# One transformer block on one core: scores of two head pairs joined, the last feed-forward columns packed, first values copied by ScalarE, orders laid anew

## What is computed

```python
scores = jnp.einsum('bqgre,bkge->bgrqk', q, k) / jnp.sqrt(jnp.float32(D_HEAD))
scores = jnp.where(causal_mask, jnp.float32(-1000000.0), scores)
probs = jax.nn.softmax(scores, axis=-1)
z = jnp.einsum('bgrqk,bkge->bqgre', probs, v)
...
h = h @ w1 + b1
a, g = jnp.split(h, 2, axis=-1)
h = a * jax.nn.gelu(g, approximate=False)
x = x + h @ w2 + b2
```

## Time and profile before

| | value |
|---|---|
| median of the runs | 1151.18 us |
| the profiled execution's own time | 1151.44 us |
| its span in the trace | 1149.6 us |
| TensorE instructions (matmul, weight load) | 17504, 17504 |
| granted TensorE clock, mean | 0.998 of full speed |
| VectorE, ScalarE, GpSimd busy | 1040.9, 1001.2, 958.5 us |

### The profile page before, as it was taken

The page is one execution under the profiler, slowest core; times in us unless marked ns, Lnnn a source line. Parts: engine busy times, 40 slices in busy tenths (PEclk is TensorE's granted clock), DMA queues, the critical chain, the costliest instruction groups (busy, mean ns, idle before and its releaser), DMA issues.

```text
span 1149.6 us, 45236 instructions
## 1 busy us (share of the span) xinstructions
PE 1132.4 (98%) x17504; PEld 820.2 (71%) x17504; DVE 1040.9 (91%) x4019; ACT 1001.2 (87%) x3168; POOL 958.5 (83%) x950
## 2 busy tenths in 40 slices
PE   9999999999999999999999999999999999999987
PEld 7677666777678676777676776777767777666765
DVE  7898899999999899999989899998998989999984
ACT  6888889888899889889898998989888898997795
POOL 2787888889888898888978889888978898988855
PEclk9999999999999999999999999999999999999999
DMA  6001010000110100111001101001001010011010
GB/s 233 11 12 33 16 32 22 21 16 9 31 27 5 45 14 3 41 25 39 14 3 36 38 23 32 17 4 42 9 23 26 4 28 23 14 35 29 11 33 27
DMA packets 31094, 31.85 MB, mean 28 GB/s; under 512 B 12576, under 2 KB 21408, under 8 KB 30752
## 3 DMA queue, kind: packets, MB, share of 16 engines
q1 hardware_dynamic: 30448, 28.17, 9.3%
q10 hardware_dynamic: 432, 0.79, 0.2%
HBM read 10.07 MB, written 2.10 MB: 11 GB/s over the span
## 4 chain that ended last, share of the span: by engine, by line
PE 83%; DVE 6%; POOL 5%; issue 2%; ACT 2%; DMA 0%; SPq 0%; POOLq 0%; DVEq 0%; ACTq 0%
PE psum L496 39%; PE psum L535 11%; PE psum L571 11%; PE psum L548 7%; PE psum L649 5%; PE psum L680 4%; PE psum L631 2%; PE psum L664 2%; DVE prob L898 1%; POOL x_hat L1164 1%; POOL rnorm L1135 1%; PE psum L594 1%; DVE b_prob L980 1%; ACT b_prob L803 1%; POOL b_prob L1152 1%
## 5 line engine op out<-in xcount | busy, mean ns | idle before, releaser
L747 ACT ACTIVATE prob<-prob,negmax 128x512 f32<-128x512 f32 (+3 forms) x512 | 282.7, 558 | 16.1 <-DVE negmax L898 15.3
L898 DVE CUSTOM_DVE_ANT_0 prob<-psum,causal 128x512 f32<-128x512 f32 (+3 forms) x512 | 224.0, 484 | 11.5 <-PE psum L535 9.6
L1102 POOL TENSOR_SCALAR prob<-prob,rowinv 128x384 f32<-128x384 f32 (+1 forms) x256 | 161.2, 649 | 50.1 <-DVE rowinv L904 48.7
L803 ACT ACTIVATE b_prob<-b_prob,b_negmax 128x128 f32<-128x128 f32 x512 | 199.0, 395 | 0.8 <-DVE b_negmax L980 0.7
L496 PE MATMUL psum<-wqkv,h_t 128*64 128x512 f32 x768 | 190.8, 599 | 0.1
L535 PE MATMUL psum<-k_t,q_t 64*128 64x384 f32 (+3 forms) x1024 | 163.5, 443 | 0.7 <-DVE prob_t L910 0.6
L1122 POOL TENSOR_TENSOR r<-r 128x512 f32<-128x512 f32 x120 | 153.4, 1284 | 7.0 <-DVE r L938 6.9
L571 PE MATMUL psum<-prob_t,v 128*64 128x256 f32 x1280 | 153.1, 380 | 0.0
L980 DVE CUSTOM_DVE_ANT_0 b_prob<-psum,band,rnorm 128x128 f32<-128x128 f32 x512 | 145.8, 344 | 5.4 <-PE psum L649 4.9
L1152 POOL TENSOR_TENSOR b_prob<-b_prob,b_rowinv 128x1024 f32<-128x1024 f32 x61 | 116.0, 1902 | 27.7 <-DVE b_rowinv L1000 27.6
L1105 POOL TENSOR_TENSOR prob<-prob,rowinv 128x512 f32<-128x512 f32 x96 | 98.1, 1047 | 36.4 <-DVE rowinv L904 36.3
(11 more groups left out here) (104 smaller groups left out, 2725.6 us busy)
## 6 DMA issues: line engine op xcount, KB each, us to landing
vb_mid<-vb SPq DMA_DIRECT2D x112, 128.0 KB, 2.4
x_t<-in_x_t SPq DMA_DIRECT2D x8, 256.0 KB, 3.9
x_n<-in_x SPq DMA_DIRECT2D x8, 256.0 KB, 3.1
x<-x SPq DMA_DIRECT2D x64, 31.8 KB
out<-x SPq DMA_DIRECT2D x15, 128.0 KB, 1.8
wqkv<-in_wqkv SPq DMA_DIRECT2D x1, 1536.0 KB, 11.3
w<-in_w SPq DMA_DIRECT2D x1, 768.0 KB, 13.1
x<-x SPq DMA_DIRECT2D x48, 0.2 KB
```

The source lines that it names most:

```text
L747: last = af(pr, pr, ACT.Exp, bias=negmax[:, k % 4, o:o + 1], scale=-1.0, accum_out=rowsum[:, k % 4, o:o + 1])
L803: last = af(pr, pr, ACT.Exp, bias=b_negmax[:, a, o:o + 1], scale=-1.0, accum_out=b_rowsum[:, a, o:o + 1])
L898: vec.tensor_tensor_reduce(prob[:, k % PROBS, h, p * K:(p + 1) * K], bank[:, p * K:(p + 1) * K], causal[:, S - K:S], -E ** -0.5, 3.0e38, A ...
L1102: last = gp.tensor_scalar(pr, pr, rowinv[:, k % 4, h:h + 1], 1.0, ALU.mult, ALU.mult)
```

## The change

Scores at i = 0 and i = 1 (`JOINT`): two head pairs, even and odd, share their keys. Of the last 64 keys only the tile's late 64 queries see any. The late queries of both pairs are copied side by side into a new tile `q_late`, and one product computes both against the last 64 keys. For each two pairs and row half there are now 3 products of 64 streamed columns at i = 0 (before: 2 of 128), and one of 192 and four of 64 at i = 1 (before: 2 of 256). All the products of one row half now come first, then those of the other. To make the outputs fit, the even pair's queries are projected with the tile's halves swapped, a second causal mask is stored, the maxima read the odd pair's blocks in another order, and `value` streams 128 columns for each pair instead of 256 for two.

Feed-forward: of the third chunk's 85 value columns, 64 are computed as one product whose two column halves take half of the tokens each, and the other 21 come out of the gate product, whose weights have room from column 96 on. `gate` of that chunk is three VectorE instructions.

`project_v` is copied out of PSUM by ScalarE. `q_late` takes one further copy on each of the two engines at i = 0 and 1. The lists of all engines, the banks and the `warm` counts are laid anew. Each step occurs as often as before, but for the `warm` steps (13 for 11, with 33 products for 34); the copy of `project_v` moves from VectorE's list to ScalarE's. In TensorE's list scores and turns of stage a now mostly alternate.

```diff
+REST = 96
...
 PROBS, PROB_TS, V_RING = 3, 4, 6
+JOINT = (0, 1)
...
-WARM = (3, 2, 2, 4, 2, 4, 3, 2, 1, 9, 2, )
+WARM = (2, 1, 1, 3, 4, 3, 3, 3, 2, 1, 5, 1, 4, )
...
-        causal = sb("causal", [P, S], BF16)
+        causal = sb("causal", [P, 2, S], BF16)
...
+        q_late = sb("q_late", [P, len(JOINT), CA // 2, P])
...
+        def even_at(i, p):
+
+            return p // 2 * 3 * E + E if i == 0 else 0
+
+        def odd_at(i, p, block):
+
+            return p // 2 * 3 * E if i == 0 else (6 - block) * E
+
+        def late_of(bank):
+
+            return bank.rearrange("p (d x n) -> p d x n", d=2, n=E)[:, :, ::3, :]
...
                 bank, = claim("a_q", b, i, h)
+                tokens = x_t[:, b % 2, i * P:(i + 1) * P]
+                turned_tokens = tokens.rearrange("p (q n) -> p q n", q=2)[:, ::-1, :]
                 for c in range(4):
-                    last = halves(bank[:, c * P:(c + 1) * P], wq[:, 4 * h + c, :], x_t[:, b % 2, i * P:(i + 1) * P])
+                    moving = turned_tokens if i in JOINT and c % 2 == 0 else tokens
+                    last = halves(bank[:, c * P:(c + 1) * P], wq[:, 4 * h + c, :], moving)
...
                 banks = claim("a_scores", b, i, c)
-                for p in range(np_):
+                queries = q_t[:, (NT * b + i) % 2, :, :]
+                for p in range(0, np_, 2 if i in JOINT else 1):
+                    keys = k_t[:, b % 2, (c + p) // 2, 0:K]
                     for h in range(2):
-                        last = mm(banks[h][:, p * K:(p + 1) * K], q_t[half(h), (NT * b + i) % 2, c + p, :],
-                                  k_t[half(h), b % 2, (c + p) // 2, 0:K], start=True, stop=True)
+                        if i not in JOINT:
+                            last = mm(banks[h][:, p * K:(p + 1) * K], queries[half(h), c + p, :], keys[half(h)], start=True, stop=True)
+                            continue
+                        even, odd = queries[half(h), c + p, :], queries[half(h), c + p + 1, :]
+                        both = q_late[half(h), i, (c + p) // 2, :]
+                        place = even_at(i, p)
+                        mm(banks[h][:, place:place + K - E], even, keys[half(h), 0:K - E], start=True, stop=True)
+                        mm(banks[h][:, place + K - E:place + K], both, keys[half(h), K - E:K], start=True, stop=True)
+                        for x in range(2 * i + 1):
+                            at = odd_at(i, p, x)
+                            last = mm(banks[h][:, at:at + E], odd, keys[half(h), x * E:(x + 1) * E], start=True, stop=True)
...
-                for p in range(0, max(np_, 2), 2):
+                for p in range(0, max(np_, 2), 1 if i in JOINT else 2):
                     for j in range(i + 1):
                         for h in range(2):
                             g = 2 * ((c + p) // 2) + h
-                            last = mm(bank[half(h), p * P:(p + 2) * P], v[:, (NT * b + j) % V_RING, g * E:(g + 1) * E],
-                                      two_pairs(k % PROB_TS, np_, i, h, p, j), start=(j == 0), stop=(j == i))
+                            values = v[:, (NT * b + j) % V_RING, g * E:(g + 1) * E]
+                            if i in JOINT:
+                                place, turned_probs = slice(p * P, (p + 1) * P), two_pairs(k % PROB_TS, np_, i, h, p - p % 2, j)[:, p % 2, :, :]
+                                if p % 2 == 0:
+                                    turned_probs = turned_probs[:, ::-1, :]
+                            else:
+                                place, turned_probs = slice(p * P, (p + 2) * P), two_pairs(k % PROB_TS, np_, i, h, p, j)
+                            last = mm(bank[half(h), place], values, turned_probs, start=(j == 0), stop=(j == i))
                 last.then_inc(valued, 1)
 
...
                 bank, = claim("b_ffn", l, g, ch)
-                for part in (1, 0):
-                    last = halves(bank[:, (1 - part) * z:(2 - part) * z], w1[:, l, part, ch * P:(ch + 1) * P], f_t[:, 0:z])
+                last = halves(bank[:, 0:z], w1[:, l, 1, ch * P:(ch + 1) * P], f_t[:, 0:z])
+                if ch < CH - 1:
+                    last = halves(bank[:, z:2 * z], w1[:, l, 0, ch * P:(ch + 1) * P], f_t[:, 0:z])
+                else:
+                    for w in range(2):
+                        last = mm(bank[half(w), z:z + z // 2], w1[:, l, 0, ch * P:ch * P + E], f_t[:, w * z // 2:(w + 1) * z // 2], start=True, stop=True)
                 last.then_inc(ffn_done, 1)
...
-                copy(q_t[:, (NT * b + i) % 2, 4 * h:4 * h + 4, :].rearrange("p c n -> p (c n)"), bank).then_inc(q_act, 1)
+                last = copy(q_t[:, (NT * b + i) % 2, 4 * h:4 * h + 4, :].rearrange("p c n -> p (c n)"), bank)
+                if i in JOINT:
+                    last = copy(q_late[:, i, 2 * h:2 * h + 2, :].rearrange("p d (x n) -> p d x n", n=E), late_of(bank))
...
+            def project_v(b, i):
+                act.wait_ge(v_done, nth("pe", "a_v", (b, i)))
+                bank, = banks_of("a_v", b, i)
+                copy(v[:, (NT * b + i) % V_RING, :], bank).then_inc(v_ready, 1)
...
-                vec.tensor_copy(q_t[:, (NT * b + i) % 2, 4 * h:4 * h + 4, :].rearrange("p c n -> p (c n)"), bank).then_inc(q_dve, 1)
-
-            def project_v(b, i):
-                dve.wait_ge(v_done, nth("pe", "a_v", (b, i)))
-                bank, = banks_of("a_v", b, i)
-                vec.tensor_copy(v[:, (NT * b + i) % V_RING, :], bank).then_inc(v_ready, 1)
+                last = vec.tensor_copy(q_t[:, (NT * b + i) % 2, 4 * h:4 * h + 4, :].rearrange("p c n -> p (c n)"), bank)
+                if i in JOINT:
+                    last = vec.tensor_copy(q_late[:, i, 2 * h:2 * h + 2, :].rearrange("p d (x n) -> p d x n", n=E), late_of(bank))
+                last.then_inc(q_dve, 1)
...
                 for p in range(np_):
                     o = h * np_ + p
-                    vec.tensor_tensor_reduce(prob[:, k % PROBS, h, p * K:(p + 1) * K], bank[:, p * K:(p + 1) * K], causal[:, S - K:S],
+                    masked, seen, mask = prob[:, k % PROBS, h, p * K:(p + 1) * K], bank[:, p * K:(p + 1) * K], causal[:, 0, S - K:S]
+                    if i in JOINT and p % 2 == 0:
+                        seen, mask = bank[:, even_at(i, p):even_at(i, p) + K], causal[:, 1, S - K:S]
+                    elif i in JOINT:
+                        masked, mask = masked.rearrange("p (x n) -> p x n", n=E), mask.rearrange("p (x n) -> p x n", n=E)
+                        if i == 0:
+                            seen = bank[:, even_at(0, p - 1) - E:even_at(0, p - 1) + K].rearrange("p (x n) -> p x n", n=E)[:, ::2, :]
+                        else:
+                            masked, mask = masked[:, ::-1, :], mask[:, ::-1, :]
+                            seen = bank[:, K - E:2 * K - E].rearrange("p (x n) -> p x n", n=E)
+                    vec.tensor_tensor_reduce(masked, seen, mask,
                                              -E ** -0.5, 3.0e38, ALU.add, ALU.min, negmax[:, k % 4, o:o + 1]).then_inc(max_ready, 1)
...
+            def gated(gelu, value, bias):
+
+                return vec.scalar_tensor_tensor(out=gelu, in0=value, scalar=bias, in1=gelu, op0=ALU.add, op1=ALU.mult)
+
             def gate(l, g, ch):
                 k, z = MCH[ch], SIZE[g] * P
                 dve.wait_ge(gelu_done, nth("act", "b_gelu", (l, g, ch)))
                 bank, = banks_of("b_ffn", l, g, ch)
-                vec.scalar_tensor_tensor(out=u_t[0:k, ch, 0:z], in0=bank[0:k, z:2 * z], scalar=b1[0:k, l, 0, ch:ch + 1],
-                                         in1=u_t[0:k, ch, 0:z], op0=ALU.add, op1=ALU.mult).then_inc(u_ready, 1)
+                if ch < CH - 1:
+                    last = gated(u_t[:, ch, 0:z], bank[:, z:2 * z], b1[:, l, 0, ch:ch + 1])
+                else:
+                    for w in range(2):
+                        gated(u_t[0:E, ch, w * z // 2:(w + 1) * z // 2], bank[half(w), z:z + z // 2], b1[half(w), l, 0, ch:ch + 1])
+                    last = gated(u_t[E:k, ch, 0:z], bank[REST:REST + k - E, 0:z], b1[REST:REST + k - E, l, 1, ch:ch + 1])
+                last.then_inc(u_ready, 1)
...
+    causal = np.stack([causal, np.roll(causal, E, 0)], 1)
...
+    w1[:, :, 1, 2 * P + REST:2 * P + REST + HID - 2 * P - E] = w1[:, :, 0, 2 * P + E:HID]
...
+    b1[:, 1, 2 * P + REST:2 * P + REST + HID - 2 * P - E] = b1[:, 0, 2 * P + E:HID]
+    b1[:, 0, 2 * P + E:] = b1[:, 0, 2 * P:2 * P + E]
```

More of the change, by code:

```diff
@@ L134 @@
-    "dve": (
[L135 to L148, removed]
-        "otusrlggogewmmgggrsAAdmihmtggglnuAoihertnlmmuwowerimsmndiwnsgwggAsgggdAdgggAd"),
@@ new lines @@
+    "47302517603514726051437260143572145721304572130456137204136720154723106547230514723560412753602753160271356047213604"
+    "72150367426156031074312065743125701562345701735235041670417624035174206352417506371053624710356150327460346701524307"
```

(14 more changed lines are left out.)

121 lines of the change are left out of this document (65 added, 56 removed), and 3 rows, old and new, of the table LETTERS.

## The result

The changed kernel takes 1194.15 us (median of four runs, 1193.57 to 1196.0) against 1151.5 for the kernel before in the same job: ratio 1.0373, 95% interval 1.0355 to 1.0391. It is 42.7 us slower, where 14 were forecast. Its profiled execution took 1194.7 us.

The account below looks back on a forecast made before the run. TensorE was taken to bound the kernel until 1050 us. Feed-forward -6.8, value +0.4, joined scores +18.7, shape changes +0.8 and late gates +1 gave +14.1 on 1151.4: 1165 us; 8-in-10 range 1142 to 1194, likeliest case 1158 to 1172.

Parts of the forecast that it names:

- The failed step: Joined scores, all products of one half issued first: the halves still overlap, nothing lost; with no overlap at all, +79 us.
- Rival A: Joined scores: engine looks only past some three waiting matmuls, +47 in place of +18.7, 1193 us; chance 20%, 3 for no overlap.
- the 1225 us: Joined scores: no overlap of the row halves at all, +79 us; chance 3%, within the 20% of Rival A.
- The load of 128 weight columns at 0.112 us a round: Joined scores: weight load sets a 64-column round's price; +7.2 us at i = 0, +11.5 at i = 1, together +18.7.
- the 0.056 of leaving: Scores steps on TensorE: a fixed cost of 0.056 us for leaving the scores, paid by each step before and after.
- The feed-forward's products: Third chunk's value product on TensorE, half the streamed columns: 6.4 us less in two-tile groups, 0.4 in one-tile, together -6.8.
- Value at i = 0 and 1: Value products on TensorE: each round of 256 columns becomes two of 128, 192 times 0.002, +0.4 us.
- Both stay under TensorE's work, which hides them until 1050 us: 0.: VectorE at 1049 us and ScalarE at 1026 stay hidden behind TensorE until 1050 us, so their added work costs 0.
- The copies and gates themselves: VectorE: v copies -21.6, q_late copies +6.7, third-chunk gates +22.6, sum +8 us of work.
- Rival B: Joined scores: streamed columns set the price, as in the transposes; -3.2 us there, 1144 us in all; chance 16%.
- rival C: Another engine becomes the bound, only as waits between lists: +3 to +10 us over the forecast; chance 8%.

Follow-up runs that it names:

- turns of one: The changed kernel with its two row halves taking turns product by product at i = 0 and 1, same products and lists: 1168.19 us, 1.0151.

## Why the prediction was wrong, point by point

The medians give the shares: 42.7 = 26.0 (order, the change less turns of one) + 14.8 (more products, turns of one less no joined scores) + 1.9 (all else). By the ratios of the jobs they are 25, 15 and 2. The forecast had put down 0, 19.1 and -5.0 for them (18.7 for the joined scores and 0.4 for value; feed-forward, lists and gates for the last): 14.1 in all.

- **The failed step** is the one in the joined scores: "I take no loss as the likeliest, since the engine does search past waiting work and 9 is not far from 3, and keep the loss as a rival." It was 26.0 us wrong. Three kernels with 6, 8 and 10 matmuls of a half in a row show the other half's start with exactly three still waiting, and 4 in a row cost 1.9 us in the whole kernel. The earlier trace rows showed a look past three and nothing beyond it; I took this least value for a hint that the true one lay higher. Of the 26 us, 22.1 are in the scores' own steps (20.8 at i = 1, 1.3 at i = 0). The other 4 are in the steps behind them, which inherit a half that is still busy, nearly all in transposes: those of the local probabilities +1.2, of the local queries and keys +1.1, turns at i = 3 +1.0, the turn ahead of the feed-forward +0.9.
- **Rival A** had the mechanism. Its time, 1193 us, is so close by luck, since its parts are off both ways: it gave 47 us for load and order at the scores, which measure 37.5 (7.8 at i = 0 where 11 were forecast, 29.7 at i = 1 where 36 were), and nothing for the steps behind them or for the other engines' work. Its arithmetic gave 1.99 us for the i = 1 step, which takes 1.82: it counted the overlap at the seam, but not that the next step's transposes start beside the last three matmuls as well. The Trainium skill ("TensorE: Matmul & The Clock Gate", Part 3) has matmuls start strictly in program order; the start at 526.63 disagrees, and the 1225 us that followed from it did not come.
- **The load of 128 weight columns at 0.112 us a round** was right: in turns of one, 12 rounds take 1.34 us at i = 0, and 2 of 0.164 with 8 of 0.112 take 1.22 at i = 1. The term came to 15.6 us in the steps (6.3 + 9.3) for 18.7, because I also charged the 0.056 of leaving in each of 48 steps (2.7 us); the joined scores don't pay it. The load records of the new products still have a mean of 188 ns, those of the transposes 139, as in the earlier trace rows:

```profile
L577 PEld LDWEIGHTS psum<-ident,prob 64*128 64x128 f32 x2560 | 99.4, 139 | 29.1 <-issue 24.7 <-POOL prob L1166 1.7 <-POOL prob L1169 0.2
L565 PEld LDWEIGHTS psum<-k_t,q_t 64*128 64x128 f32 x512 | 66.2, 188 | 0.0
L562 PEld LDWEIGHTS psum<-k_t,q_late 64*128 64x128 f32 x256 | 40.8, 188 | 0.0
```

- **The feed-forward's products** were right: -5.8 us for two tiles (forecast 6.4) and -0.5 for one (0.4). The new value product (L742) takes 0.22 us, 601.82 less 601.60:

```profile
601.60 0.39 PE L742 MATMUL psum<-f_t,w 128*64 128x128 f32 x4
601.82 1.03 PE L511 MATMUL psum<-wqkv,h_t 128*64 128x512 f32 x4
```

- **Value at i = 0 and 1**: right. -0.1 us against the kernel before, but +0.5 against the kernel without joined scores, which has the same lists (0.873 for 0.863 a step, in 48 steps), for +0.4.
- **"Both stay under TensorE's work, which hides them until 1050 us: 0."** was wrong. The copies and gates themselves were priced rightly (+8.5 us by their rows for +8; VectorE's busy time rose by 16, since many other instructions take a few ns more), but not what they do. Without the joined scores the feed-forward's products save 6.3 us and the kernel is 1.9 slower, so lists, copies and gates cost 8.2 where 1.8 were put down. What such work costs depends on the lists around it. The packed feed-forward puts 23 to 24 us more on VectorE in three pairs of kernels and should save 6.3 in products: in the old lists it gives back 15, in the old lists with ScalarE's copy of v 11, in the new lists with that copy 3 to 4. ScalarE's copy costs 6 in the old lists. The trace puts only part of it into a named wait: TensorE waits for u_t for 2.9 us in the changed kernel against 0.7 before.

```profile
PE psum L511 <- DVE u_t L1094: 2.9, 6, 0.9
```

- **Rival B** is out, **rival C** (+3 to +10) was true beside A, not instead of it.

Left open: the half of the lost 15 us that shows as longer steps and not as a named wait, and what makes the same work cost 15 us in one set of lists and 4 in the other. Moving the longest gate away from the end of its group changed nothing or made it worse. What part of the 4.6 us belongs to the lists' order and what to ScalarE's copy stays open too: that copy costs 6 us in the old lists by itself, so the new lists may be fitting it rather than adding to it.

No kernel here beats the kernel before. The nearest is the one without joined scores, 0.1 to 0.3% slower.

## What to carry over

Where two halves of the array can work side by side, let them alternate matmul by matmul, and count matmuls, not products: against turns of one product (two matmuls), four in a row of one half cost this kernel 1.9 us, blocks of up to six 14, blocks of six and ten 26. Splitting a product to save streamed columns pays only while the stream is longer than the load of its weights: with 128 weight columns a round of 64 streamed columns cost 0.108 us here and one of 128 cost 0.112, so a column saved was worth nothing, and each further product cost a load. An engine at 91% busy beside one at 98% is not free: price what is added to it with an experiment that adds only that, in the lists in which it is to run.

## What the runs showed of the chip that I had not expected

- The other half's first matmul starts when exactly three of the first half's still wait: after 7 of 10, 5 of 8 (in the kernel before with its order changed; 0.51 us after the step's start), 3 of 6. With 4 in a row the median i = 1 step of the kernel before stays at 0.92 us.
- An engine with idle time for 9% of the span still passes added work on, and how much hangs on the lists: 23 to 24 us on VectorE gave back 15, 11 or 3 to 4 us, 18 on ScalarE 6.
- A gate's time hung on its columns and not on its rows: 21 rows of 256 columns take 491 ns, 85 take 472; 64 rows of 128 columns take 344, 128 rows 341.
